# A transformer layer on one core: rows of y laid out by DMA, a ring of queries of two chunks and a ring of exponentials of four quads

## The reference

```python
xn = layernorm(x)
Q, K, V = split(xn @ Wqkv); Q, K = rope(Q), rope(K)            # 16 heads of 8 numbers
attn = softmax(where(causal, Q @ K^T / sqrt(8), -inf))          # per head, 1024 x 1024
y = (attn @ V) with the heads side by side                      # 128 numbers a row
mlp = silu(xn @ Wg + bg) * (xn @ Wu + bu) @ Wd + bd
experts = a retrieval of 8 of 512 experts per head (top_k over sums of key scores, softmax, silu)
return x + y @ Wproj + mlp + experts
```

## Time and profile before

| | us |
|---|---|
| runs: median of 3 (lowest, highest) | 770.66 (767.44, 770.99) |
| the profiled execution: its own time | 770.97 |
| its span, first to last instruction | 769.2 |

### The profile page before, as it was taken

One profiled execution on the slowest core, in us unless ns is written; L12 is line 12 of the kernel. 1 busy time (PEld: TensorE's weight loads), 2 busy tenths in 40 slices (PEclk: granted clock), 3 DMA queues, 4 the chain that ended last, 5 costly groups with the idle time before them and its releaser, 6 DMA issues.

```text
span 769.2 us, 15222 instructions
## 1 busy us (share of the span) xinstructions
PE 688.9 (90%) x5756; PEld 280.9 (37%) x5756; DVE 613.1 (80%) x1292; ACT 539.0 (70%) x824; POOL 414.4 (54%) x547
## 2 busy tenths in 40 slices
PE   3976688898889899999798999999999999999997
PEld 2442133333333434443233343443233433333343
DVE  4569989999878998998688996789966799784532
ACT  3342166259999768637698776574988668999982
POOL 5463277477887795378357615158400136764840
PEclk9988579899999999999999999999999999999999
DMA  6536003133000010025400002520300001000000
GB/s 140 103 63 86 3 1 42 31 55 71 1 2 1 1 31 28 3 38 68 90 2 1 5 1 32 74 48 16 56 2 2 1 1 31 3 1 4 2 1 28
DMA packets 33814, 22.48 MB, mean 29 GB/s; under 512 B 6380, under 2 KB 33388, under 8 KB 33740
## 3 DMA queue, kind: packets, MB, share of 16 engines
q1 hardware_dynamic: 32876, 20.72, 15.7%
q10 hardware_dynamic: 864, 0.79, 0.6%
HBM read 6.23 MB, written 2.10 MB: 11 GB/s over the span
## 4 chain that ended last, share of the span: by engine, by line
PE 42%; DVE 23%; ACT 10%; issue 8%; POOL 8%; DMA 4%; SPq 3%; ACTq 1%; POOLq 0%; DVEq 0%
DVE pmax L1115 14%; PE ybank L1350 10%; PE banks L1382 7%; ACT pT L965 6%; PE banks L1327 6%; DVE wsum L1183 4%; PE banks L1403 4%; PE banks L1298 4%; SPq L677 3%; PE banks L1275 2%; POOL ssum L829 2%; ACT wsum L1008 2%; POOL coef L846 2%; DMA qs<-negmaxT 2%; PE banks L1336 2%
## 5 line engine op out<-in xcount | busy, mean ns | idle before, releaser
L1115 DVE TENSOR_REDUCE pmax<-banks 128x2 f32<-128x1024 f32 (+3 forms) x304 | 344.3, 1161 | 42.1 <-PE banks L1308 24.0
L965 ACT ACTIVATE pT<-banks 128x1024 f32<-128x1024 f32 (+3 forms) x384 | 295.8, 830 | 57.8 <-PE banks L1336 39.0
L829 POOL TENSOR_TENSOR ssum<-sim 128x512 f32<-128x512 f32 x128 | 144.8, 1136 | 123.0 <-DVE wsum L1183 63.1
L1350 PE MATMUL ybank<-pT,vaug 128*32 128x512 f32 (+3 forms) x1536 | 167.0, 510 | 0.7 <-ACT pT L965 0.2
L1298 PE MATMUL banks<-ks,qs 48*128 48x512 bf16 (+3 forms) x768 | 117.4, 346 | 32.8 <-DVE pmax L1115 25.8
L1327 PE MATMUL banks<-qs,ks 51*128 51x512 bf16 (+3 forms) x768 | 122.9, 337 | 21.7 <-ACT pT L965 9.1
L1183 DVE SCALAR_TENSOR_TENSOR wsum<-ssum,best,wsum 128x512 f32<-128x512 f32 x128 | 122.5, 971 | 11.0 <-ACT wsum L1008 10.8
L1008 ACT ACTIVATE wsum<-ssum,wbias 128x512 f32<-128x512 f32 x128 | 92.9, 742 | 26.4 <-POOL ssum L829 21.2
L846 POOL TENSOR_TENSOR coef<-coef,wsum 128x512 f32<-128x512 f32 x64 | 87.0, 1360 | 33.8 <-DVE wsum L1183 32.7
L1327 PEld LDWEIGHTS banks<-qs,ks 51*128 51x128 bf16 x768 | 36.7, 94 | 154.9 <-ACT pT L965 107.3
L1298 PEld LDWEIGHTS banks<-ks,qs 48*128 48x128 bf16 x768 | 32.9, 96 | 129.0 <-DVE pmax L1115 71.1
(11 more groups left out here) (113 smaller groups left out, 834.4 us busy)
## 6 DMA issues: line engine op xcount, KB each, us to landing
ks<-parts SPq DMA_DIRECT2D x90, 64.0 KB
qs<-parts SPq DMA_DIRECT2D x90, 64.0 KB
xin<-in_L_attn_x SPq DMA_DIRECT2D x4, 512.0 KB, 4.8
osb<-in_L_attn_x SPq DMA_DIRECT2D x8, 256.0 KB, 2.8
out<-osb SPq DMA_DIRECT2D x8, 256.0 KB, 2.3
ks<-parts ACTq DMA_DIRECT2D x6, 64.0 KB
qs<-parts ACTq DMA_DIRECT2D x6, 64.0 KB
qs<-negmaxT SPq DMA_DIRECT2D x16, 24.0 KB
```

The source lines that it names most:

```text
L829: g.tensor_tensor(ssum[:, m % NSS, :, :], s[:, h, 0:XI].unsqueeze(2).to_broadcast([P, XI, NKEYS]), s[:, RH + h:RH + h + 1, :].to_broadcast ...
L965: a_.activation(pT[:, q % NPT, 2 * e:2 * e + 2, q0:CHUNK], pair(("sc", *n))[:, :, q0:CHUNK], ACT.Exp, scale=SCALE).then_inc(out_sem, 1)
L1115: v.tensor_reduce(pmax[:, c, i % TPC, k0 // CHUNK, :].rearrange("p (e j) -> p e j", e=2) [:, :, js[0]:js[-1] + 1], pair(("mx", b, c, k))[: ...
L1350: ins = t_.matmul(ybank[32 * j:32 * j + 32, q0:CHUNK], vaug[:, b % 2, kt, v0:v0 + 32], pT[:, q % NPT, j, q0:CHUNK], start=kt == 0, stop=kt ...
```

## The change

1. `yt`, `ym`, `yo` and `Yo` go. In their place SP copies within SBUF, for each half stage (two groups, task `yg`), the rows of y and the rows of sums from `yT4` into a tile `yz`: four DMAs of 32 KB for y, two of 64 KB that lay each sum down eight times. Once a stage DVE takes the reciprocal of all sums, 128x512, and multiplies, 128x512 (task `yd`). `Wproj` is loaded with its rows in the order in which y then lies.
2. A `Yc` waits for the DMAs of the group pair before, not for `yt`.
3. `NPT = 4`, `NQS = 2`.
4. All five lists are written anew.

```diff
-NPT = 3
-NQS = 3
+NPT = 4
+NQS = 2
...
+                elif kind == "yg":
+                    c, two = n
+                    for gr in (2 * two, 2 * two + 1):
+                        w.wait_ge(done["Yc"], rank("Yc", b, c, gr))
+                    if serial(b, c) > 0:
+                        w.wait_ge(done["ac"], rank("ac", *STAGES[serial(b, c) - 1], NF))
+                    r = HALF * two
+                    for j in range(4):
+                        sp.dma_start(yz[r + 2 * DH * j:r + 2 * DH * (j + 1), 0, :], yT4[32 * j:32 * j + DH, :, :])\
+                            .then_inc(y_rows_loaded, 16)
+                    for e in range(2):
+                        sp.dma_start(yz[r + e:r + HALF:2, 1, :],
+                                     yT4[DH::32, e, :].unsqueeze(1).to_broadcast([4, DH, CHUNK]))\
+                            .then_inc(y_rows_loaded, 16)
...
                     if k >= 2:
-                        w.wait_ge(done["yt"], rank("yt", *GROUP_ORDER[k - 2]))
+                        w.wait_ge(y_rows_loaded, y_rows(*GROUP_ORDER[k - 2]))
                     a_.activation(yT4[:, k % 2, :], ybank[:, :], ACT.Copy).then_inc(out_sem, 1)
...
+                elif kind == "yd":
+                    b, c = n
+                    for gr in range(GROUPS):
+                        w.wait_ge(y_rows_loaded, y_rows(b, c, gr))
+                    s = mark(v.reciprocal(yz[:, 1, :], yz[:, 1, :]))
                     need(s)
-                    v.tensor_tensor(ytm[:, :, 4 * gr:4 * gr + 4, :], wv[:, :, :, 0:DH],
-                                    yinv[:, k % 2, :, :].unsqueeze(3).to_broadcast([P, TPC, 4, DH]), ALU.mult)\
-                        .then_inc(out_sem, 1)
+                    v.tensor_tensor(yT, yT, yz[:, 1, :], ALU.mult).then_inc(out_sem, 1)
```

More of the change, by code:

```diff
@@ new lines @@
+gt.1.1.3@5 mx.2.0.2@23 gt.1.1.2@4 mt.1.1@1 gt.1.1.1@6 mx.2.0.3@23 mx.2.0.4@01 sm.2.1@5 up.1.1.2@6 up.1.1.3@4
+mx.2.0.5@23 sc.1.1.0.0.0@01 up.1.1.0@5 up.1.1.1@6 sc.1.1.0.0.1@01 sc.1.1.0.1.0@23 mx.2.0.6@45 sc.1.1.0.1.1@01
+pv.1.1.0.0 sc.1.1.0.2.0@23 mx.2.0.7@45 sc.1.1.0.2.1@01 pv.1.1.0.1 sc.1.1.0.3.0@23 sc.1.1.0.3.1@01 pv.1.1.0.2
+mx.2.0.8@45 sc.1.1.0.4.0@23 sm.2.2@6 sc.1.1.0.4.1@01 mx.2.0.9@45 sc.1.1.0.5.0@23 pv.1.1.0.3 mx.2.0.10@45
+sc.1.1.0.5.1@01 sc.1.1.0.6.0@23 pv.1.1.0.4 sc.1.1.0.6.1@01 sc.1.1.0.7.0@23 mx.2.0.11@45 pv.1.1.0.5 sc.1.1.0.7.1@01
@@ new lines @@
+sc.2.1.2.6.0@01 pv.2.1.2.4 sc.2.1.2.6.1@23 sc.2.1.2.7.0@01 mx.3.1.26@45 pv.2.1.2.5 pv.2.1.2.6 sc.2.1.2.7.1@01
+sc.2.1.3.0.0@23 mx.3.1.27@45 ct.2.1.2@6 sc.2.1.3.0.1@01 pv.2.1.2.7 mx.3.1.28@23 sc.2.1.3.1.0@45 sm.3.6@6
+sc.2.1.3.1.1@01 mx.3.1.29@23 sc.2.1.3.2.0@45 pv.2.1.3.0 sc.2.1.3.2.1@01 mx.3.1.30@23 pv.2.1.3.1 sc.2.1.3.3.0@45
+sc.2.1.3.3.1@01 mx.3.1.31@23 pv.2.1.3.2 sc.2.1.3.4.0@45 mx.3.1.32@23 sc.2.1.3.4.1@01 pv.2.1.3.3 sc.2.1.3.5.0@23
+mx.3.1.33@45 sc.2.1.3.5.1@01 pv.2.1.3.4 sc.2.1.3.6.0@23 sc.2.1.3.6.1@01 mx.3.1.34@45 pv.2.1.3.5 mx.3.1.35@23
@@ new lines @@
+up.3.1.0@6 sc.3.1.0.1.0@01 sc.3.1.0.1.1@23 pv.3.1.0.0 sc.3.1.0.2.0@01 mx.3.0.0@45 sc.3.1.0.2.1@23 pv.3.1.0.1
+sc.3.1.0.3.0@01 mx.3.0.1@45 sc.3.1.0.3.1@23 sm.3.0@6 sc.3.1.0.4.0@01 mx.3.0.2@45 sc.3.1.0.4.1@23 pv.3.1.0.2
+sc.3.1.0.5.0@01 pv.3.1.0.3 sc.3.1.0.5.1@23 pv.3.1.0.4 sc.3.1.0.6.0@01 sc.3.1.0.6.1@23 pv.3.1.0.5 mx.3.0.3@45
+sc.3.1.0.7.0@01 sc.3.1.0.7.1@23 pv.3.1.0.6 sc.3.1.1.0.0@01 sc.3.1.1.0.1@23 mx.3.0.4@45 pv.3.1.0.7 sc.3.1.1.1.0@01
+mx.3.0.5@45 sc.3.1.1.1.1@23 pv.3.1.1.0 sc.3.1.1.2.0@01 mx.3.0.6@45 sc.3.1.1.2.1@23 pv.3.1.1.1 mx.3.0.7@45
@@ new lines @@
+pv.3.0.2.1 sc.3.0.2.3.1@01 sc.3.0.3.0.0@23 pv.3.0.2.2 sc.3.0.3.0.1@01 pv.3.0.2.3 sc.3.0.3.1.0@23 ac.3.1.5
+sc.3.0.3.1.1@01 sc.3.0.3.2.0@23 ac.3.1.6 sc.3.0.3.2.1@01 ac.3.1.7 sc.3.0.3.3.0@01 sc.3.0.3.3.1@23 pv.3.0.3.0
+pv.3.0.3.1 pv.3.0.3.2 pv.3.0.3.3 ac.3.1.8 gt.3.0.3@5 dn.3.0.2@4 ot.3.1@6 dn.3.0.1@3 dn.3.0.3@5 ct.3.0.2@6 ct.3.0.1@4
+ct.3.0.3@5 dn.3.0.0@3 gt.3.0.0@6 ct.3.0.0@5 gt.3.0.2@4 gt.3.0.1@6 up.3.0.3@5 up.3.0.2@4 up.3.0.0@6 up.3.0.1@5
+ac.3.0.0@6 ac.3.0.1 ac.3.0.2 ac.3.0.3 ac.3.0.4 ac.3.0.5 ac.3.0.6 ac.3.0.7 ac.3.0.8 ot.3.0@6
@@ L339 @@
[L339 to L342 removed]
+st.0 wp.1 wp.0 xv.0.1 xv.0.3 xv.0.2 xv.0.0 rp.0.0.1 rv.0.0.1 rp.0.0.0 v1.0.0.1 rv.0.0.0 st.1 v1.0.0.0 v2.0.0.1
@@ L592, in build @@
         NFIRST = 3
-        NWEIGHTS = 11
+        NWEIGHTS = 12
         NCONST = 3
@@ L613, in rank, with y_rows @@
             return RANK[task]
+        def y_rows(b, c, gr):
+            return 16 * 6 * (GROUP[b, c, gr] // 2 + 1)
         def rows(b, c, a):
@@ L1352, in _ @@
                     ins.then_inc(out_sem, 1)
-                elif kind == "yt":
-                    b, c, gr = n
-                    w.wait_ge(done["Yc"], rank("Yc", b, c, gr))
-                    for m in range(TPC):
-                        ins = t_.transpose(single(task)[:, m * P:(m + 1) * P],
-                                           yT4[:, GROUP[b, c, gr] % 2, m * P:(m + 1) * P], ident[:, :])
-                    ins.then_inc(out_sem, 1)
-                elif kind == "yo":
-                    b, c = n
-                    for gr in range(GROUPS):
-                        w.wait_ge(done["ym"], rank("ym", b, c, gr))
-                    for m in range(TPC):
-                        ins = t_.transpose(single(task)[:, m * P:(m + 1) * P],
-                                           ytm[:, m, :, :].rearrange("p h d -> p (h d)"), ident[:, :])
-                    ins.then_inc(out_sem, 1)
                 elif kind == "sm":
```

595 lines of the change are left out of this document (279 added, 316 removed), and 7 rows, old and new, of the table KINDS.

## The result

| | before | after |
|---|---|---|
| median of the runs, us | 769.84 | 801.88 (798.75 to 804.15) |
| ratio to before, 95% interval | | 1.0418 [1.0368, 1.0467] |
| span of the profiled execution, us | 769.2 | 798.4 |

The account below looks back on a forecast made before the run. The bound changes by stage: DVE in (0,0), PE in (2,1), ACT in (3,1), the rest between. Terms 4.6 - 16.4 + 20.3 - 8.3 + 16.8 - 7.1 + 4.9 - 3.9 = +10.9 on 770.97 gave 782 us, range 757 to 800.

Parts of the forecast that it names:

- The reciprocals' weight: On DVE, `yd` takes 3.8 us, 1.6 more a stage than what it replaces; hidden in (2,1).
- Rival 2: On DVE, the reciprocal is as cheap as a product: 14.5 us off at six places, 767.5 us; chance 0.20.
- PE's win: PE loses 40 transpose groups, 21.6 us to win where PE is the bound; (2,1) -7.1, (3,0) -3.9 us.
- (0,1): Stage (0,1): 20 maxima fewer, ACT becomes the bound, 75 us at 97% is 77: -16.4 us.
- The start: Stretch before (0,0): same work within 2 us, change 0.
- Theory S: Forecast for e3: the start's extra 5.2 us come from `st.2` waiting for rows before the first maxima; 797 to 798 us.
- DVE's work in the long stages: DVE work 96.8 us in (0,0), +4.6; behind lead-ins 89.0 in (1,0), +20.3, and 87.4 in (2,0), +16.8.
- the price of the operation: On DVE, a reciprocal of 128x512 takes 3.1 us, scaled from one row of 16 numbers.
- the length of the lead-ins: Beginnings of (1,0) and (2,0) without maxima, waiting for rows of y and `yd`: 21 and 19 us, DVE nearly idle.
- (1,1) and (3,1): Both bound by ACT: (1,1) 67.1 us at 97%, -8.3; (3,1) 66.0 us at 98%, +4.9.
- Rival 1: PE sets the pace throughout: all 21.6 us of transposes come off, 749 us; a stretch under 83 us decides; chance 0.13.
- Rival 3: Rows of y land 7 us later at three places, PE and ACT stand: +21, 803 us; chance 0.12.

Follow-up runs that it names:

- e1: Kernel after without the reciprocal in `yd`, its product kept (division left out): 773.5 us, 1.0065 of before.
- e5: Lists and rings of before, with y by DMA and `yd` with its reciprocal in place of the transposes: 796.4 us, 1.0353 of before.
- e7: Lists and rings of before, with y by DMA and only the product of `yd`, no reciprocal: 770.9 us, 1.0012 of before.
- e10: Kernel before with y left out behind its first copy, no transposes, DMA copies or `yd`: 766.5 us, 0.9927 of before.
- e3: Kernel after with the third batch's statistics, inverse root and normalization moved out of the start to later: 807.6 us, 1.0514 of before.
- e8: Kernel after with the inverse on ACT as exp(-ln), `yd.3.0` behind `hu.3.0.1`, `yl.2.0` and three `yd` moved later: 780.4 us, 1.0171 of before.
- e11: Kernel after with seven of eight reciprocals cut into four pieces of 128 columns, other work between: 802.7 us, 1.0440 of before.
- e2: Kernel after with the inverse on ACT as exp(-ln), only the product on DVE, `yd.3.0` behind `hu.3.0.1`: 790.4 us, 1.0270 of before.
- e9: Kernel before with every transpose of y issued twice into the same bank: 778.5 us, 1.0136 of before.
- e12: Kernel before, y by PE as it was, with seven more unneeded reciprocals of 128x512 on DVE: 786.4 us, 1.0228 of before.
- e4: Order and rings of after, with the old way of y by PE transposes put back: 804.4 us, 1.0459 of before.

## Why the prediction was wrong

The direction and the pattern were right; five terms of the sum were not, and one of these errors hid part of the others.

1. **The reciprocals' weight.** I charged them at six places, 14.5 us in all above the price of a product, which is 18.6 against no reciprocal (six times 3.1), and wrote that in (2,1) "`yd` is hidden, DVE having 78 us of work in 95". They cost 28.4 (after to e1) and 25.5 (e5 to e7). DVE's free time in a stage is no cover: in (2,1) of after, DVE's maxima wait 15.0 of its 23.2 free us for PE's products, and while DVE divides, PE waits for banks, as around the first `yd` above. Of the forecast's miss of 18.3 us over the stages, (2,1) is 9.4, and the reciprocal there is 3.7 of it; the end is 7.7, and the reciprocal there cost 5.1, where I had allowed 1.5 for `yg` and `yd` together. Rival 2 was the right question: it asked what this operation is worth, but gave it 7 to 10 us too little.

2. **PE's win.** "So 40 x 0.54 = 21.6 us are PE's to win, where PE is the bound", and -7.1 for (2,1) because PE was busy 98% of it. This is the largest part of the miss, 5.7 in (2,1) and 4.1 at the end: PE's lost maxima and transposes were to win 7.1 and 5.4 there, and even in e1, without the reciprocals, the two are only 1.4 and 1.3 shorter than before. e7 took the groups out of (2,1) in the order of before and the stage became 0.4 us shorter; e10 puts all of them, DVE's and ACT's part included, at 5.6. In (2,1) of e7 PE is 2.2 us less busy than before and waits longer instead, 1.9 us for banks in place of 0.6. My last sentence on it, that the win "is real; it is lost because PE's and DVE's work are taken apart", is wrong in both halves. The second falls by the pairs: (0,1), (1,0), (1,1) and (2,0) took 357.9 us together in e1 and 360.0 in e7, one with the order of after and the other with that of before. Of the +12.4 that I had forecast for them, 10.1 of the 12.6 measured are the four reciprocals in them, and not the order.

3. **(0,1).** I let ACT set it at 77 (75 at 97% is 77.3, so my -16.4 should have been -16.0). It took 83.5 and was no shorter in e1. POOL has 72 us there and is busy 99% of the last 33.5; e3 put 8.9 us more on it and lost 8.3. The bound is shown by the trace and by e3; 3.5 of the 83.5 go with the lower clock (80.0 in e8 and e11).

4. **The start.** Forecast 0, measured +5.2. All runs with the lists of after but one have their first score of (0,0) between 95.5 and 97.3 (e2 at 100.0), those with the lists of before between 89.6 and 92.0, so it belongs to the order of the setup. The two traces split it. PE's first products of the first pass start at 51.1 instead of 47.5 (+3.6). In after the products that make the values stand in front of those that make the queries, and the first copy of query rows is issued at 36.5 instead of 31.0; that the one causes the other is not shown. The first maximum starts 5.5 us after those first products instead of 1.3 (+4.2): the third batch's statistics stand in front of it and DVE waits 6.8 us for their rows. From there to the first score it is 39.3 instead of 41.9 (-2.6), with 30 maxima in place of 34. e3 took the statistics away, and the first maximum came 1.3 us after the products, as Theory S has it; but in its profiled execution these started only at 55.5, as in e2 (55.6), whose start is that of after. So what the statistics cost in the median stays open.

5. **DVE's work in the long stages.** In (0,0) and behind the lead-ins of (1,0) and (2,0) I counted 96.8, 89.0 and 87.4 us for DVE; it was busy 92.2, 83.1 and 81.1, and the stages came out 11.7 shorter than forecast together. The windows of after, lead-in and stretch of maxima in (1,0), then in (2,0):

```profile
277.50:299.10 21.60, 18.11 (x194) 7.86 (x192) 16.22 (x50) 18.94 (x37) 21.43 (x33) 0.92 0.50 74
299.10:384.90 85.80, 80.58 (x558) 31.32 (x556) 83.06 (x92) 48.73 (x66) 28.38 (x30) 1.00 0.23 42
455.60:476.60 21.00, 18.63 (x182) 8.38 (x178) 17.25 (x52) 17.70 (x35) 16.11 (x25) 1.00 0.47 81
476.60:562.20 85.60, 76.76 (x513) 29.30 (x514) 81.10 (x90) 41.43 (x58) 21.01 (x23) 0.94 0.22 40
```

The lead-ins are about as long as forecast, 21.6 and 21.0 (21 and 19), but DVE is busy 16.2 and 17.3 us of them and not nearly idle, and the stretches are 85.8 and 85.6 (91.8 and 90.1), with DVE at 97% and 95%.

What held: the price of the operation, the direction, the length of the lead-ins, DVE at 95% or more behind them, and (1,1) and (3,1) within 1.5. Rival 1, PE's pace, asked for a stretch under 83 (85.8 measured) and is answered by e7 and e10: there is no such win even without the reciprocals. Rival 3, late rows, did not come: `yd` waited 1.4 us in all, and no `Yc` waited for a copy.

So the 32 us are the reciprocals' 28.4, and some 5 in which the order of after is a little worse than that of before (start +6.8 and (3,1) +4.5, against -5.3 in (0,0), e1 beside e7) and PE's lost transposes give next to nothing back; the two come from different sets of runs and add up to a little more. Still open: why work taken away in e7 and e10 gives so little when the same kind of work, added in e9 and e12, costs 44% (e9, 0.24 of 0.54) to 74% (e12, 2.5 of 3.35) of its length, and the reciprocals, taken away in e1, gave back all of theirs. The lists were written for the work as it was: those of before have places for the transposes, those of after have none, and there e4 pays 31 us over e1. That this is the reason is not shown; no run here wrote the lists anew for less.

## What to carry to other kernels

Before an operation is moved, ask how many numbers a partition it will then work on: the sums were 16 a partition behind the transposes and 512 behind the DMA that lays each down eight times, and a reciprocal pays by the number. In a kernel whose engines hand banks to each other in fixed order, price an added piece at most of its length on whichever engine empties the banks (74 to 106% here), even where that engine is busy only 80%, and price a piece removed from another engine, as PE's transposes here, at little until a run that leaves it out has shown more. For every stage of a forecast, work out all engines, the quiet one too: in (0,1) it was POOL.

## What the runs showed of the hardware

The reciprocal on DVE grew with the numbers of a partition in a straight line: 0.25 us for 16, 0.94 for 128 (e11), 3.35 for 512, so (3.347 - 0.940) / 384 = 6.3 ns a number and some 0.14 us fixed. The Trainium skill (VectorE: DVE Perf Modes, "First, the fixed hardware budget") gives the divide operations of a reciprocal a repeat count of 8; read as eight cycles a number that made the estimate of 4.3 us in the prediction, and the trace, at 3.35, does not agree.

The same inverse as ln and exp on ACT took 0.63 us for each of the two activations of 128x512, 1.26 together, against 3.35 on DVE.

PE's busy share did not say what a removed step would win: with 160 transposes fewer PE was busy 19.3 us less over an equal span (e7), and in (2,1) it still showed 98.0 of 101.5.
